# Two attention layers in one kernel: scores turned before the exponential, row sums by TensorE

## The reference

```python
# layer 0: attention to the context, 16 heads of 8 channels, with biases; then eight experts, the best two per token
x = x + tanh(g_xattn[0]) * L0_xattn(layernorm(x), ctx, wq, bq, wk, bk, wv, bv, wo, bo)
x = x + tanh(g_ffn[0])   * L0_experts(layernorm(x), w1, w2, router_w)
# layer 1: attention without biases or output weights, a padding mask on the queries; then channel mixing
x = x + tanh(g_xattn[1]) * L1_xattn(layernorm(x), ctx, mask, Wq, Wkv)
x = x + tanh(g_ffn[1])   * L1_mixing(layernorm(x), W_r, W_k, W_v, mu_r, mu_k)

def attention(q, k, v):                       # per head
    scores = q @ k.T / sqrt(8)                # 128 queries x 77 keys
    p = exp(scores - max(scores, axis=-1))
    return (p / p.sum(axis=-1)) @ v
```

## Time and profile before

| what | us |
|---|---|
| median of three runs (360.46 to 363.15) | 362.51 |
| span of the profiled execution, first to last instruction | 379.8 |
| busy in it: TensorE | 301.1 |
| busy: VectorE | 267.3 |
| busy: ScalarE | 204.3 |
| busy: GpSimd | 212.2 |

### The profile page before, as it was taken

How to read it: one execution, slowest core, us unless ns; L and a number is a source line. 1 busy time by engine, 2 the same in 40 slices (tenths; PEclk the granted TensorE clock), 3 DMA queues, 4 the chain that set the end, 5 groups by cost and what they waited for, 6 DMA issues and landing times.

```text
span 379.8 us, 7644 instructions
## 1 busy us (share of the span) xinstructions
PE 301.1 (79%) x2230; PEld 212.8 (56%) x2230; DVE 267.3 (70%) x747; ACT 204.3 (54%) x534; POOL 212.2 (56%) x398
## 2 busy tenths in 40 slices
PE   3995999787797778478899948759878987696874
PEld 3673655555465458466678737536545554454653
DVE  0464899989997966453454416668979899698574
ACT  3633788566663633323455514347666767486622
POOL 7238665554786746472000165655676876986381
PEclk9998799899896995666999988966898889698789
DMA  4880991000000002111232233210000000000012
GB/s 113 229 215 28 437 413 59 0 2 3 15 30 14 30 28 76 37 56 29 77 84 73 83 91 84 63 37 14 16 14 16 22 22 2 0 2 3 2 37 74
DMA packets 27189, 24.97 MB, mean 66 GB/s; under 512 B 5316, under 2 KB 25485, under 8 KB 26637
## 3 DMA queue, kind: packets, MB, share of 16 engines
q1 hardware_dynamic: 25101, 20.28, 16.6%
q0 software_dynamic: 2048, 4.20, 3.9%
HBM read 9.92 MB, written 14.55 MB: 64 GB/s over the span
## 4 chain that ended last, share of the span: by engine, by line
DVE 31%; PE 28%; issue 12%; POOL 8%; ACT 8%; another core or an unknown queue 3%; DMA 0%; SPq 0%; POOLq 0%; DVEq 0%; ACTq 0%
DVE pr L469 8%; DVE mx L441 7%; DVE smm L486 5%; PE scores_ps L1446 5%; ACT pr L422 4%; PE bank L1428 3%; PE bank L294 2%; PE bank L1429 2%; PE bank L1430 2%; PE bank L1437 2%; PE scores_ps L356 2%; DVE xrn L1042 1%; POOL rstd L107 1%; PE scores_ps L1412 1%
## 5 line engine op out<-in xcount | busy, mean ns | idle before, releaser
L422 ACT ACTIVATE pr<-pr 128x512 f32<-128x512 f32 (+1 forms) x96 | 51.9, 551 | 22.6 <-DVE pr L469 22.3
L1530 POOL DMA_INDIRECT back<-expert_rows,row_of x32 | 31.4, 980 | 57.6 <-DMA expert_rows<-w_sb 42.9
L294 PE MATMUL bank<-ident,pr 128*128 128x128 f32 x320 | 59.9, 317 | 0.5
L383 ACT COPY pT<-bank 128x512 f32<-128x512 f32 (+1 forms) x96 | 47.7, 516 | 13.3 <-PE bank L294 10.4
L356 PE MATMUL scores_ps<-kbd,work 32*128 32x308 f32 x256 | 38.8, 530 | 16.7 <-DVE pr L469 15.8
L441 DVE TENSOR_REDUCE mx<-scores_ps 128x8 f32<-128x616 f32 x64 | 47.7, 787 | 5.3 <-PE scores_ps L356 5.3
L469 DVE TENSOR_TENSOR pr<-scores_ps,mx 128x512 f32<-128x512 f32 (+1 forms) x96 | 48.8, 564 | 0.1
L294 PEld LDWEIGHTS bank<-ident,pr 128*128 128x128 f32 x320 | 44.9, 165 | 6.2 <-ACT work L413 4.3
L1479 DVE TENSOR_TENSOR w_sb<-w_sb,bank 128x256 f32<-128x256 f32 x39 | 16.4, 420 | 38.3 <-ACT w_sb L1458 29.0
L486 DVE TENSOR_REDUCE smm<-pr 128x16 f32<-128x1024 f32 x32 | 39.0, 1218 | 4.5 <-ACT pr L422 4.5
L343 PE MATMUL bank<-pT,vbd 128*32 128x128 f32 x768 | 39.2, 308 | 1.6 <-ACT pT L383 1.6
(11 more groups left out here) (241 smaller groups left out, 656.4 us busy)
## 6 DMA issues: line engine op xcount, KB each, us to landing
expert_rows<-back SPq DMA_DIRECT2D x4, 2048.0 KB, 13.7
w_sb<-expert_rows SPq DMA_DIRECT2D x39, 64.0 KB
expert_rows<-w_sb SPq DMA_DIRECT2D x39, 64.0 KB
w_sb<-in_L_ffn_w_dram SPq DMA_DIRECT2D x4, 512.0 KB, 6.1
xs<-in_x_dram SPq DMA_DIRECT2D x4, 256.0 KB, 3.8
w_sb<-in_L_ffn_w_dram SPq DMA_DIRECT2D x4, 256.0 KB, 6.7
out_dram<-xs SPq DMA_DIRECT2D x3, 256.0 KB, 2.3
expert_rows<-xrn,row_of POOLq DMA_INDIRECT x32
```

The lines of the kernel that those rows point to most:

```text
L294: mm = pe.transpose(ps[:, c0 + P * i:c0 + P * i + P], pr[:, u, P * c:P * c + P], ident[:])
L383: act.copy(pT[:, 4 * P * n:4 * P * n + P * len(chunks)], ps[:, c0:c0 + P * len(chunks)]).then_inc(pT_ready, 1)
L422: act.activation(part, part, ACT.Exp, scale=SCALE).then_inc(exp_done, 1)
L1530: pool.indirect_dma_start(back[:, b, k, :], None, xrow, bass.IndirectOffsetOnAxis(ap=row_of[:, b, k:k + 1], axis=0)).then_inc(gathered[b % ...
```

## The change

- The shifted scores, not the probabilities, are turned by TensorE, in the slot of the shift. ScalarE's exponential reads them in PSUM and writes `pT`: the three copies and the exponentials in SBUF become three exponentials.
- The sums of rows come from TensorE: with `ones_bd`, blocks of ones in the place of the values, twelve more matmuls a tile sum the same turned probabilities into `s_ps`, beside `o_ps` in one bank. VectorE's two sums and GpSimd's addition go.
- In layer 0 VectorE divides in a chain of its own (`divide`): it turns the sums within 32 x 32 blocks, takes the reciprocal, turns it back, spread over the channels, and multiplies the output. GpSimd's spreading, TensorE's turning and ScalarE's copy of it go. In layer 1 the sums travel with the output: ScalarE copies both, TensorE turns both, ScalarE reads both to `tmp`, VectorE takes the reciprocal from there in the next slot.
- TensorE's slot has a new order: scores of tile t; in layer 1 the output of tile t - 2; transposes of tile t - 1, the input of tile t + 1 turned in between; in layer 0 the output of tile t - 2; query of tile t + 1; weighing of tile t - 1. Input and query are a slot earlier than before, ScalarE's `normalise` two slots ahead of the scores.
- Layer 1's gate is multiplied into the value weights in the setup; the gates are loaded under a semaphore of their own, and the tanh is taken before that copy. GpSimd builds `ones_bd` in the setup.

The core of the diff (buffers, renamings and the setup's load list left out):

```diff
-            xn_ps, rT_ps = bank[0][:, 0:P], bank[0][:, P:2 * P]
-            o_ps, out_ps = bank[1][:, 0:P], bank[1][:, P:2 * P]
-
-            q_ps = xn_ps if layer == 0 else rT_ps
-
-            GROUPS = [(bank[2], 0, range(0, CM, 2)), (bank[3], 0, range(1, CM, 2)), (bank[0], 2 * P, range(CM, CH))]
-            def t_after(t, n):
-                return t >= n
+            xn_ps = q_ps = bank[0][:, 2 * P:3 * P]
+            os_ps = bank[1][:, 0:2 * P]
+            o_ps, s_ps = bank[1][:, 0:P], bank[1][:, P:2 * P]
+            out_ps = bank[0][:, 3 * P:4 * P] if layer == 0 else bank[1][:, 2 * P:4 * P]
+
+            GROUPS = [(bank[0], range(CM, CH)), (bank[2], range(0, CM, 2)), (bank[3], range(1, CM, 2))]
+            REST, EVEN, ODD = range(3)
...
-                    if stage(t, 2):
-                        pool.wait_ge(part_sum, 2 * (t - 1))
-                        pool.tensor_tensor(sm[:, u, :], smm[:, u, :], smr[:, u, :], ALU.add).then_inc(sum_ready, 1)
...
+                def transpose_in(t):
+                    pe.wait_ge(xn_ready, t + 1)
+                    pe.transpose(xn_ps, xn[:, t % 2, :], ident[:]).then_inc(xnT_done, 1)
+
+                def query(t):
+                    pe.wait_ge(xnT_ready, t + 1)
+                    pe.matmul(q_ps, wq0_sb[:] if layer == 0 else wq1T[:], xnT[:, t % 2, :],
+                              start=True, stop=True).then_inc(q_done, 1)
+
                 def transpose_chunks(u, n):
-                    ps, c0, chunks = GROUPS[n]
+                    ps, chunks = GROUPS[n]
                     for i, c in enumerate(chunks):
-                        mm = pe.transpose(ps[:, c0 + P * i:c0 + P * i + P], pr[:, u, P * c:P * c + P], ident[:])
+                        mm = pe.transpose(ps[:, P * i:P * i + P], pr[:, u, P * c:P * c + P], ident[:])
                     mm.then_inc(pT_done, 1)
 
+                def weigh(u, n):
+                    for dst, first in ((o_ps, n == REST), (s_ps, False)):
+                        for j in range(RG):
+                            if n == REST:
+                                w, c, ones = CM + j, CM + j // 2, 2 + j % 2
+                            else:
+                                w, c, ones = 2 * j + n - EVEN, 2 * j + n - EVEN, n - EVEN
+                            left = vbd[:, u, 32 * w:32 * w + 32] if dst is o_ps else ones_bd[:, ones, :]
+                            k = 8 + j // 2 if n == REST else 4 * (n - EVEN) + j
+                            mm = pe.matmul(dst[32 * j:32 * j + 32, :], left, pT[:, P * k:P * k + P],
+                                           start=first, stop=(n == ODD), skip_group_check=True)
+                    return mm
...
-                    before_out(pe, t)
-                    if stage(t, 2):
-                        pe.wait_ge(oT_ready, t - 1)
-                        if layer == 0:
-                            pe.matmul(out_ps, oT[:, u, :], wo_tg[:], start=True, stop=True
+                    if layer == 1:
+                        before_out(pe, t)
+                        if stage(t, 2):
+
+                            pe.wait_ge(oT_ready, t - 1)
+                            for i in range(2):
+                                mm = pe.transpose(out_ps[:, P * i:P * i + P], oT[:, u, P * i:P * i + P], ident[:])
+                            mm.then_inc(out_done, 1)
+                    if stage(t, 1):
+                        pe.wait_ge(shifted, 3 * t)
+                        if stage(t, 2):
+                            pe.wait_ge(pT_ready, 3 * (t - 1))
+                        if stage(t, 0):
+                            pe.wait_ge(q_ready, t + 1)
+                        if stage(t, 3) and layer == 0:
+                            pe.wait_ge(out_read, t - 2)
+                        transpose_chunks(1 - u, REST)
+                        transpose_chunks(1 - u, EVEN)
+                    if stage(t, -1) and stage(t, 0):
+                        if stage(t, 1):
+                            pe.wait_ge(pT_ready, 3 * (t - 1) + 1)
+                        transpose_in(t + 1)
+                    if stage(t, 1):
+                        transpose_chunks(1 - u, ODD)
+                    if layer == 0:
+                        before_out(pe, t)
+                        if stage(t, 2):
+                            if stage(t, 1):
+                                pe.wait_ge(pT_ready, 3 * (t - 1) + 1)
+                            if stage(t, -1):
+                                pe.wait_ge(xnT_ready, t + 2)
+                            pe.wait_ge(oT_ready, t - 1)
+                            pe.matmul(out_ps, oT[:, u, 0:P], wo_tg[:], start=True, stop=True
                                       ).then_inc(out_done, 1)
-                        else:
-                            pe.transpose(out_ps, oT[:, u, :], ident[:]).then_inc(out_done, 1)
+                    if stage(t, -1) and stage(t, 0):
+                        query(t + 1)
+                    if stage(t, 1):
+
+                        pe.wait_ge(vbd_ready, 2 * t)
+                        if stage(t, 2):
+                            pe.wait_ge(oT_ready, t - 1)
+                            if layer == 1:
+                                pe.wait_ge(out_read, t - 1)
+                        for n in range(3):
+                            pe.wait_ge(pT_ready, 3 * (t - 1) + n + 1)
+                            mm = weigh(1 - u, n)
+                        mm.then_inc(pv_done, 1)
 
                 before(pe)
+                transpose_in(0)
+                query(0)
...
+                def exponentials(t, n):
+                    ps, chunks = GROUPS[n]
+                    lo = 8 * P if n == REST else 4 * P * (n - EVEN)
+                    act.wait_ge(pT_done, 3 * t + n + 1)
+                    act.activation(pT[:, lo:lo + P * len(chunks)], ps[:, 0:P * len(chunks)], ACT.Exp,
+                                   scale=SCALE).then_inc(pT_ready, 1)
+
...
+                def read_out(u, t):
+                    act.wait_ge(out_done, t - 1)
+                    if stage(t, 4):
+                        act.wait_ge(res_done, t - 3)
+                    width = D if layer == 0 else 2 * D
+                    act.copy(tmp[:, u, 0:width], out_ps).then_inc(out_read, 1)
...
+                    if stage(t, 2) and layer == 1:
                         act.wait_ge(pv_done, t - 1)
+                        act.copy(oT[:, u, :], os_ps).then_inc(oT_ready, 1)
+                        read_out(u, t)
+                    if stage(t, 1):
+                        if stage(t, 2):
+                            act.wait_ge(pv_done, t - 1)
+                        exponentials(t - 1, REST)
+                    if stage(t, -1) and stage(t, 0):
+                        columns(t + 1)
+                    if stage(t, 1):
+                        exponentials(t - 1, EVEN)
+                        exponentials(t - 1, ODD)
+                    if stage(t, -1) and stage(t, 0):
+                        query(t + 1)
+                    if stage(t, 2) and layer == 0:
+                        read_out(u, t)
+                    if stage(t, -2) and stage(t, 0):
+                        if layer == 1 and t % 2 == 0:
+                            act.wait_ge(experts_rstd, t // 2 + 2)
                         act.wait_ge(xnT_done, t + 1)
+                        normalise(act, t + 2)
...
+                def divide(u, t):
+
+                    dve.wait_ge(pv_done, t - 1)
+                    dve.transpose(sumq[:], s_ps).then_inc(sumq_ready, 1)
+                    dve.wait_ge(sumq_ready, t - 1)
+                    dve.reciprocal(rc[:, u, :], sumq[:].rearrange("p (k d) -> p k d", d=DH)[:, :, 0]
+                                   ).then_inc(recip_ready, 1)
+                    dve.wait_ge(recip_ready, t - 1)
+                    dve.transpose(rT[:], rc[:, u, :].unsqueeze(2).to_broadcast([P, H, DH])).then_inc(rT_ready, 1)
+                    dve.wait_ge(rT_ready, t - 1)
+                    dve.tensor_tensor(oT[:, u, 0:P], o_ps, rT[:], ALU.mult).then_inc(oT_ready, 1)
...
-                    if stage(t, 2):
-                        dve.wait_ge(sum_ready, t - 1)
-                        if layer == 1 and stage(t, 4):
-                            dve.wait_ge(out_scaled, t - 3)
-                        dve.reciprocal(rc[:, u, :], sm[:, u, :]).then_inc(recip_ready, 1)
+                    if stage(t, 3) and layer == 1:
+                        dve.wait_ge(out_read, t - 2)
+                        if stage(t, 5):
+                            dve.wait_ge(out_scaled, t - 4)
+                        dve.reciprocal(rc[:, v, :], tmp[:, v, D:2 * D].rearrange("p (h d) -> p h d", d=DH)[:, :, 0]
...
+                    if stage(t, 2) and layer == 0:
+                        divide(u, t)
                     after_shift(dve, t)
-                    if stage(t, 1):
-                        dve.wait_ge(exp_done, 3 * (t - 1) + 1)
-                        if stage(t, 3):
```

(26 more changed lines are left out.)

171 lines of the change are left out of this document (37 added, 134 removed).

## The result

| | runs | median, us | lowest to highest |
|---|---|---|---|
| before | 4 | 362.83 | 360.46 to 364.1 |
| after | 4 | 347.89 | 344.16 to 349.98 |

The ratio of after to before is 0.9551, with a 95% interval of 0.9468 to 0.9635. Ratios and their intervals leave out slow runs, those over 1.5% above the fastest of their kernel, which the medians take in. The forecast was 341, the range 328 to 358; 347.89 lies in the range and 2 us above the likeliest case's own 336 to 346. The profiled execution of after took 348.58 us, its span is 346.9.

A forecast was written before the change was run, and what follows sets the result against it. VectorE was taken as nearest to full in both layers' attention. Six savings summed to 22.4 us, taking the profiled 379.8 to 357.4, times 0.9545 giving 341 us; range 328 to 358.

The forecast's parts named there:

- the likeliest case: Whole kernel: the forecast's own outcome of 341 us, 336 to 346, chance 0.48.
- three quiet slots: Layer 0's slots without routing: from 5.02 to 4.6 to 4.7 us each, saving 1.2 us (0 to 2).
- ten routing slots: Layer 0's slots that also carry routing: VectorE saves 0.7 us each, 7 in all; 4 taken between 0 and 7.
- layer 0's start: Only the third tile's keys hold: its scores at 42.5, maxima at 43.0 in place of 46.22, saving 3.2 us.
- layer 0's end, to the experts' first block: Exponentials and weighing come in the last tile's shift slot, division in the next: 3 us saved (0 to 4).
- layer 1's fifteen slots: Slots fall from 6.1 to 5.5 us, with a third of the time at 1.2 GHz: 9 us saved (0 to 18).
- layer 1's end: Last tile's transposes and weighing come a slot earlier, ahead of the mixing: 2 of 3.9 us saved (0 to 4).
- The sum of 22.4: All six savings in us of the profiled execution: 1.2 + 4 + 3.2 + 3 + 9 + 2.
- the two sums (4.7 and 4.3): Quiet slot's work in us: TensorE 4.7 after overlap of block ends, VectorE 4.3, at most 5.1.
- the rival at 2.4 GHz: TensorE keeps 2.4 GHz in layer 1, GpSimd sets 4.9 us a slot: 18 saved there, 333 us; chance 0.18.
- GpSimd takes VectorE's place: Layer 1: ScalarE's input scaling waits for GpSimd's scale of pairs; 2 us saved in place of 9, 348 us; chance 0.17.
- The scale of 0.9545: Whole kernel: median without a profile, 362.51 us, over the profiled span, 379.8; turns 357.4 into 341.

The follow-up runs named there:

- second profile of before: The kernel before, unchanged, run and profiled again: 361.18 us, span 359.5.
- first profile of before: The profiled execution of the unchanged kernel before that the forecast read: span 379.8 us, with 125.57 over the experts.
- second profile of after: The changed kernel, unchanged, run and profiled again as reference: 347.16 us, ratio to before 0.9535.
- The fill: TensorE turns the identity where it waits, added to after with output's turn first, layer 1's statistics later, heads' product on VectorE: 331.86 us, ratio to before 0.9125.

## Why the prediction was right in range and 7 us low

By its own steps, in us of the profiled execution, gains as measured between the second profile of before and the two of after:

| step | forecast | measured |
|---|---|---|
| three quiet slots | 1.2 | 1.2 |
| ten routing slots | 4 | 2.2 to 3.2 |
| layer 0's start | 3.2 | 0.6 (1.2 to 1.3 against the first profile of before) |
| layer 0's end, to the experts' first block | 3 | -1.1 to 0.7 |
| layer 1's fifteen slots | 9 | 10.5 to 13.7 |
| layer 1's end | 2 | -4.0 to -4.8 |

The sum of 22.4 stands against 12.6 and, with the second profile of after, 16.1. That the result fell into a range 30 us wide is in part luck: four of the six steps are off, and what layer 1's slots gave above the forecast covered a part of what its end and layer 0's start and end didn't give.

*Quiet slots: right.* 4.6 us each, the forecast's 4.6 to 4.7. VectorE's transposes took 0.31 to 0.32 where 0.30 was taken, and 0.03 to 0.04 lies between the four steps where 0.05 was. TensorE and VectorE meet, as the two sums (4.7 and 4.3) had it: 4.52 and 4.35 busy. TensorE's sum of 4.88 was a little high, since its 1.08 for the scores holds a wait; eight such matmuls take 0.80 where nothing holds them (45.24 below).

*Routing slots: right in kind, near the middle.* VectorE's busy time fell by 7.4 us, the forecast's 7; more than half became waits, as the step feared. What it left out is the level: the grant over the stretch is 0.90, and filling TensorE's waits there gave 2.8 us back. With the grant near full the ten slots differ by 0.9 us with and without the division, so that little of their length hung on VectorE's work.

*The start: the step that failed first.* It said that only the keys of the third tile hold, with its scores at 42.5 and its maxima at 43.0. The timeline of after:

```profile
39.37 1.90 PE L309 MATMUL scores_ps<-kbd,work 32*128 32x308 f32 x8 [1.13 <-DVE pr L471]
...
43.15 1.12 ACT L379 ACTIVATE pT<-bank 128x512 f32<-128x512 f32 x2
...
43.80 0.43 PE L294 MATMUL bank<-pT,vbd 128*32 128x128 f32 x8
...
44.17 0.36 ACT L388 ACTIVATE work<-bank,bq_col 128x128 f32<-128x128 f32 x1
...
45.24 0.80 PE L309 MATMUL scores_ps<-kbd,work 32*128 32x308 f32 x8
...
46.57 1.50 DVE L431 TENSOR_REDUCE mx<-scores_ps 128x8 f32<-128x616 f32 x2
```

The first maxima come 1.62 us later here than in the profile that the forecast read, so that its 42.5 and 43.0 answer to 44.1 and 44.6. The keys were there at 42.6. But the third tile's query is copied (L388) behind two exponentials of the first tile, and its scores stand in TensorE's queue behind the weighing of that tile, at 45.24; the division, which stands before the maxima, ends at 46.66. So the scores come 1.1 us late and the maxima 2.0. In the second profile of before the third tile's scores begin as long after the first maxima (8.52 us, 8.53 here), also behind the weighing. The second tile's scores take 1.90 us at the low level, as in before. The fill takes 1.4 us off, against the kernel beside it; that the order holds most of the rest is read from the timeline and wasn't tried. The forecast had used this order for the steady slot and forgotten it at the start.

*Layer 0's end: not there.* The last residual does begin earlier, 12.77 us after the last maxima (138.37 - 125.60) in place of 15.14. But the routing on which the experts wait, of the last quarter but one and then of the last, begins later. Second profile of before, last maxima at 129.10:

```profile
133.19 0.60 PE L949 MATMUL scores_ps<-ident,xrn 128*128 128x128 f32 x4
...
144.63 0.29 DVE L448 BATCH_NORM_STATS2 bns<-xs 128x6 f32<-128x128 f32 x1
```

After, last maxima at 125.60:

```profile
133.21 0.66 PE L950 MATMUL scores_ps<-ident,xrn 128*128 128x128 f32 x4
...
142.19 0.28 DVE L437 BATCH_NORM_STATS2 bns<-xs 128x6 f32<-128x128 f32 x1
```

TensorE's routing transposes come 7.6 us after the maxima in place of 4.1, as the last tile's weighing now stands before them, and the last statistics 16.6 in place of 15.5. The residual is done 3.4 us before them, but VectorE takes the routing of an earlier quarter first, and this waits for those transposes. ScalarE's first step of the experts' first block, second profile of before and after:

```profile
159.04 0.41 ACT L1464 CAST xbh<-scores_ps 128x128 fp32r<-128x128 f32 x2
156.68 0.41 ACT L1464 CAST xbh<-scores_ps 128x128 fp32r<-128x128 f32 x2
```

That is 29.9 us after the last maxima and 31.1 (29.3 in the second profile of after): no 3 us. The step counted to the residual, and what the experts wait for is the routing. The whole stretch to layer 1 took from 103.9 to 107.4 us in kernels that are the same there.

*Layer 1's slots: larger than forecast.* The step took a third of the time at 1.2 GHz, as before; the slots got denser and the grant, 0.58 over the first two, was 1.00 in all others (in the second profile it fell again in four of them). It didn't reach the 18 of the rival at 2.4 GHz: GpSimd held VectorE through the statistics, 14.9 us of waits, and with these and its product moved the slots fell to 73.24 and 72.25, 18 to 19 less than before. Of the rival "GpSimd takes VectorE's place" the time (348) came true, and GpSimd did hold the layer, but not by the way that the rival named: ScalarE's scaling waited 0.8 us on GpSimd's scale, and layer 1 saved five to seven times what it said. Which part of the gain comes from the sums that left VectorE and which from the slot that a tile's way is shorter wasn't tried. One reading was wrong: in the last of the three windows before, TensorE (15.42 of 16.20) and not VectorE (14.54) is nearest to full.

*Layer 1's end: wrong in sign.* The step counted the work that comes a slot earlier and not that the reciprocal, which the change makes depend on the turned output, is moved behind other steps in two queues. Of the 7 us between forecast and result 3.4 to 4.2 came back when these queues were reordered. The 2 us of the step didn't show even then (32.25 beside 31.67). (Against the first profile of before the step's loss is 1.4 to 2.3; its last stretch had a grant of 0.85 in place of 0.95.)

The scale of 0.9545 was needed: the first profile's extra 18 us lay in the experts, which the change doesn't touch. Between the second profile of before and the two of after the change's sum is 12.6 and 16.1 us of 359.5, or 3.5% and 4.5%; the runs have 4.5% (3.7 to 5.3).

## What to carry to other kernels

When a change turns an operand into the result of a longer chain, look at the first and last slots as well as the steady one: there its new producers and consumers stand in queues beside work that the steady slot never meets. An engine's saved time is worth what the next bound leaves: here layer 1's slots went from 5.2 us to 5.0 and then 4.8 to 4.9 as one bound after another was moved, with TensorE's 4.47 behind them. Before a shorter stretch is put down to the work that was taken out, compare the granted clock: here it explained most of what leaving out the division seemed to give. And where TensorE waits, filling the wait with idle work can pay: 1.4, 2.8 and 1.1 us in three stretches here.

## What the runs showed of the hardware

- A float32 transpose of 128 x 128 on VectorE (within blocks of 32 x 32) took 0.31 to 0.32 us, out of PSUM as well as from a broadcast operand in SBUF.
- The same slot of the same kernel took 3.62 us at a granted clock of 1.00 and 5.97 at 0.63, each time after a slot of 4.8 us with TensorE half idle. What decides whether the grant falls is open.
- Quiet slots repeat to 0.01 us from run to run (13.85 to 13.86 in seven profiles), while the experts, of the same instructions, took from 103.9 to 107.4 us in kernels that are the same there, and 125.6 in one profile of before.
